# Swin block kernel: the third bf16 part of the attention bias of unshifted blocks as two products of 64 rows

## What is computed

```python
attn = jnp.einsum('bhnd,bhmd->bhnm', q * SCALE, k)
attn = attn + rpb[RPI].transpose(2, 0, 1)[None]
if shifted:
    attn = (attn.reshape(B, NW, HEADS, N, N) + MASK[None, :, None]).reshape(-1, HEADS, N, N)
attn = jax.nn.softmax(attn, -1)
```

## Time and profile before

| | us |
|---|---|
| median of 3 runs | 988.06 |
| lowest and highest | 987.23, 990.0 |
| the profiled execution | 987.27 |
| its span, first to last instruction | 985.4 |
| mean granted TensorE clock in it | 0.865 |
| TensorE busy with products | 796.8 (81%) in 7978 |
| VectorE busy | 794.4 (81%) in 2001 |
| ScalarE busy | 574.2 (58%) |
| GpSimd busy | 244.6 (25%) |

### The profile page before, as it was taken

One profiled execution on the slowest core, in us unless ns is written; L12 is line 12 of the kernel. 1 busy time (PEld: TensorE's weight loads), 2 busy tenths in 40 slices (PEclk: granted clock), 3 DMA queues, 4 the chain that ended last, 5 costly groups with the idle time before them and its releaser, 6 DMA issues.

```text
span 985.4 us, 20394 instructions
## 1 busy us (share of the span) xinstructions
PE 796.8 (81%) x7978; PEld 535.5 (54%) x7980; DVE 794.4 (81%) x2001; ACT 574.2 (58%) x859; POOL 244.6 (25%) x272
## 2 busy tenths in 40 slices
PE   3799999999999999999999979798667655543544
PEld 1577877877777777777777764483111111121222
DVE  8788889988888998888999965744459998989842
ACT  2277777677777777777766663214667636555002
POOL 6122222222222222222222211571201221124100
PEclk8699999999999999999999998799768765565656
DMA  8200000000000000002000000100005666556300
GB/s 225 65 1 3 1 2 2 2 1 3 1 2 2 2 2 1 3 1 103 1 3 2 1 2 4 46 1 0 2 0 97 129 128 126 95 100 128 80 0 17
DMA packets 11621, 34.13 MB, mean 35 GB/s; under 512 B 1879, under 2 KB 4359, under 8 KB 11271
## 3 DMA queue, kind: packets, MB, share of 16 engines
q0 software_dynamic: 5904, 21.24, 11.4%
q1 hardware_dynamic: 5623, 11.60, 4.0%
HBM read 10.81 MB, written 0.79 MB: 12 GB/s over the span
## 4 chain that ended last, share of the span: by engine, by line
PE 62%; DVE 22%; issue 5%; ACT 5%; POOL 2%; DMA 2%; POOLq 0%; SPq 0%; DVEq 0%; ACTq 0%
PE narrow L1453 5%; PE wide L1376 4%; PE scores_a L1425 4%; PE scores_b L1425 4%; PE last L1530 4%; PE scores_a L1412 3%; PE scores_b L1436 3%; PE scores_b L1412 3%; PE scores_a L1436 3%; PE narrow L1483 3%; DVE prod L991 3%; DVE prod L999 2%; PE last L1526 2%; PE wide L1516 2%; PE last L1503 2%
## 5 line engine op out<-in xcount | busy, mean ns | idle before, releaser
L376 POOL TENSOR_TENSOR stb<-stb,neg_half 128x4 f32<-128x4 f32 x48 | 48.4, 1007 | 253.2 <-DVE stb L679 253.2
L1104 ACT ACTIVATE d<-d 128x768 f32<-128x768 f32 x96 | 80.6, 839 | 18.4 <-DVE d L626 17.9
L1453 PEld LDWEIGHTS narrow<-v,pt 128*64 128x64 f32 x2304 | 78.7, 137 | 13.4 <-issue 13.4
L1453 PE MATMUL narrow<-v,pt 128*64 128x54 f32 x2304 | 84.9, 224 | 0.1
L371 POOL TENSOR_TENSOR sta<-sta,neg_half 128x4 f32<-128x4 f32 x48 | 48.9, 1018 | 104.8 <-DVE sta L566 104.8
L1111 ACT ACTIVATE pt<-scores_a 128x768 f32<-128x768 f32 x48 | 38.9, 810 | 56.6 <-PE scores_a L1436 56.6
L1120 ACT ACT_TABLE_LOAD x47 | 60.3, 1283 | 0.8
L1104 ACT ACT_TABLE_LOAD x46 | 59.0, 1283 | 0.8
L613 DVE TENSOR_REDUCE mx<-scores_a 128x12 f32<-128x768 f32 x48 | 46.0, 958 | 16.7 <-PE scores_a L1425 16.7
L1700 PE MATMUL scores_b<-xb,gates_w 128*32 128x512 bf16 x192 | 25.7, 543 | 40.4 <-DVE yo L1013 31.7
L1120 ACT ACTIVATE ga<-wide 128x512 f32<-128x512 f32 x48 | 28.7, 598 | 48.2 <-PE wide L1516 48.2
(11 more groups left out here) (330 smaller groups left out, 2168.2 us busy)
## 6 DMA issues: line engine op xcount, KB each, us to landing
gsum<-mag POOLq DMA_DIRECT2D x14, 512.0 KB, 4.6
ysum<-yo POOLq DMA_DIRECT2D x7, 768.0 KB, 5.8
ysum<-xd POOLq DMA_DIRECT2D x6, 768.0 KB, 5.8
gsum<-mag POOLq DMA_DIRECT2D x14, 256.0 KB, 4.7
wts<-in_wpack SPq DMA_DIRECT2D x6, 442.0 KB, 7.6
sed_w<-in_sed_in SPq DMA_DIRECT2D x1, 2304.0 KB, 8.0
graw<-in_gates_in SPq DMA_DIRECT2D x1, 1152.0 KB, 5.1
x_all<-in_x_tok SPq DMA_DIRECT2D x8, 96.0 KB, 2.9
```

The source lines that it names most:

```text
L1104: act.activation(d, d, ACT.Exp).then_inc(p_ready[u], 1)
L1453: op = pe.matmul(y_ps[64 * b:64 * b + 64, q * VO:(q + 1) * VO], t.pt[:, q, h, 64 * b:64 * b + 64], t.v[:, q, b, h * VO:(h + 1) * VO], star ...
```

## The change

The third part (`bias_lm`) of an unshifted block's bias is now used in products of 64 rows: bank 0 takes rows 0 to 63 of `bias_lm` and of `ident2`, bank 1 rows 64 to 127. So the low part of the second head triple has to lie in rows 64 to 127, where the zeros were: VectorE copies it there behind `table_low` of the even blocks, after a wait for that operation, and the three memsets of zeros on GpSimd are gone. The loops of `bias` are swapped (part outside, bank inside), for shifted blocks too. `tables_done` counts the copies as well, and the counts waited for on it and on `set_v` follow.

```diff
--- before.py
+++ after.py
@@ -39,6 +39,7 @@
 T_COLS = 3456
 L_OFF = [0, 384, 1920, 2304, 3840, 4224]
 L_COLS = 5760
+TABLES = [2, 3, 5, 6, 8, 9]
 
 
 V_PROJ, V_PB, V_PCM, V_F1A, V_F1B, V_F2A, V_F2B, V_GA, V_GC, V_FB, V_YB = (int(n) for n in np.cumsum(
@@ -319,7 +320,7 @@
             for dst, src in ((conv_w[:], conv_in), (l1w[:], l1_in), (l2w[:], l2_in), (front_w[:], front_in),
                              (taps_w[:], taps_in), (l3w[:], l3_in), (spread[:], spread_in)):
                 sp.dma_start(dst, src).then_inc(ld_late, 16)
-            sp.wait_ge(tables_done, BLOCKS)
+            sp.wait_ge(tables_done, TABLES[-1])
             sp.dma_start(sed_w[:], sed_in).then_inc(ld_sed, 16)
             sp.dma_start(signs[:], sign_in).then_inc(ld_sed, 16)
             sp.wait_ge(y_act, CHUNKS)
@@ -352,17 +353,17 @@
             def set_values():
                 for t in st:
                     pool.memset(t.v[:], 0.0).then_inc(set_v, 1)
-                pool.wait_ge(set_v, 5)
+                pool.wait_ge(set_v, 2)
                 for s, t in enumerate(st):
                     for r in range(2):
                         pool.memset(sum_columns(t, r), 1.0).then_inc(set_v, 1)
-                    pool.wait_ge(set_v, 7 + 2 * s)
+                    pool.wait_ge(set_v, 4 + 2 * s)
                 for t in st:
                     pool.memset(t.on[:, :, C:C + 1], 1.0).then_inc(set_on, 1)
                     pool.memset(t.on[:, :, C + 1:64], 0.0).then_inc(set_on, 1)
                 pool.memset(zf[:, :, :, C:C + 1], 1.0).then_inc(set_on, 1)
                 pool.memset(zf[:, :, :, C + 1:64], 0.0).then_inc(set_on, 1)
-                pool.wait_ge(set_v, 9)
+                pool.wait_ge(set_v, 6)
                 pool.wait_ge(set_on, 6)
 
             def rstd_a(n):
@@ -391,9 +392,6 @@
 
             rstd_e(0)
             pool.wait_ge(emb_rstd, 1)
-            for b in (0, 2, 4):
-                pool.memset(bias_lm[64:128, L_OFF[b]:L_OFF[b] + SC], 0.0).then_inc(set_v, 1)
-            pool.wait_ge(set_v, 3)
             for k in range(SLOTS + 4):
                 if k >= 45:
                     rstd_f(k - 45)
@@ -732,6 +730,9 @@
                     low = bias_lm[0:64, L_OFF[b] + w * u:L_OFF[b] + w * (u + 1)]
                     op = dve.tensor_tensor(low, rpb_sb[:, T_OFF[b]:T_OFF[b] + w], low, ALU.subtract)
                 op.then_inc(tables_done, 1)
+                if b % 2 == 0:
+                    dve.wait_ge(tables_done, TABLES[b] - 1)
+                    dve.tensor_copy(bias_lm[64:128, L_OFF[b]:L_OFF[b] + 192], bias_lm[0:64, L_OFF[b] + 192:L_OFF[b] + SC]).then_inc(tables_done, 1)
 
             dve.wait_ge(set_ln, 15)
             embed_centre(0)
@@ -769,7 +770,7 @@
                     fill(2)
                     fill(3)
                 if k == 2:
-                    dve.wait_ge(set_v, 9)
+                    dve.wait_ge(set_v, 6)
                     dve.wait_ge(set_on, 6)
                 take_v(k - 2)
                 take_k(k - 1)
@@ -1394,22 +1395,27 @@
                     return
                 b = n // CHUNKS
                 if n % CHUNKS == 0 and u == 0:
-                    pe.wait_ge(tables_done, b + 1)
+                    pe.wait_ge(tables_done, TABLES[b])
                     if b == 1:
                         pe.wait_ge(ld_mask, 16 * 3)
                 if n >= 1:
                     pe.wait_ge(pt_ready[u], n)
-                for r in range(2):
-                    for part in range(2):
+                for part in range(2):
+                    for r in range(2):
+                        rows = slice(0, 128)
                         if shifted(n):
                             off = (T_OFF[b], L_OFF[b] + 768 * u)[part] + SC * r
                             rhs = (bias_hm, bias_lm)[part][:, off:off + SC]
                             dst = sc_bank[u][:, r, 0:SC]
                         else:
-                            off = (T_OFF[b], L_OFF[b])[part] + 192 * r
-                            rhs = (bias_hm, bias_lm)[part][:, off:off + 192].unsqueeze(1).to_broadcast([128, 2, 192])
+                            if part:
+                                rows = slice(64 * r, 64 * r + 64)
+                                rhs = bias_lm[rows, L_OFF[b]:L_OFF[b] + 192]
+                            else:
+                                rhs = bias_hm[:, T_OFF[b] + 192 * r:T_OFF[b] + 192 * r + 192]
+                            rhs = rhs.unsqueeze(1).to_broadcast([rows.stop - rows.start, 2, 192])
                             dst = sc_bank[u][:, r, 0:SC].rearrange("p (v c) -> p v c", v=2)
-                        pe.matmul(dst, ident2[:], rhs, start=(part == 0), stop=(part == 1))
+                        pe.matmul(dst, ident2[rows], rhs, start=(part == 0), stop=(part == 1))
 
             def scores(n, u):
                 if not live(n):
```

## The result

The changed kernel takes 991.02 us in the median of 22 runs, 989.58 to 997.91; the kernel before, 988.10 us (22 runs, 986.9 to 991.61). The ratio is 1.0037, with a 95% interval of 1.0024 to 1.0050: slower, by 2.4 to 4.9 us. The profiled execution has a span of 990.5 us against 985.4.

The account below looks back on a forecast made before the run. The chain was TensorE for 62% and VectorE for 22%. Terms +2.1 (scores_a), +0.3 (scores_b), +0.3 (half clock) and +0.8 (VectorE copies) sum to +3.5 us; on the median of 988.06 that gives 991.5 us, range 987.6 to 995.8.

Parts of the forecast that it names:

- case A: In TensorE's bias groups, switching between full and partial array costs 0.095 us each way; 989.6 to 992.6 us; chance 0.70.
- The change of the array: On TensorE, each switch between full products and 64-row products costs 0.095 us, twice per bias group.
- Rival B: In the scores_a group, two bf16 64-row products slip between full ones without the drain; 986.7 us; chance 0.13.
- The load of the pair: The weight load in front of the two 64-row products is uncovered for 0.01 us; 0.10 kept for the range.
- rival C: The 64-row weight load loses its short form: +0.09 us in some 43 groups, +3.9, 995.4 us; chance 0.11.
- The load behind the pair: The load for the transposes after the scores_a group adds 0.06 us; bounds 0 and 0.10.
- scores_a pays, scores_b does not: Bias groups: scores_a +0.10 us each; scores_b only +0.015, since the projection behind it waits for VectorE's copy of oT.
- 21 groups: Of 24 unshifted chunks, 21 pay for their groups: scores_a +2.1 us in all, scores_b +0.3 over some 20.
- The copies: Three VectorE copies of 0.27 us: +0.30 in the start-up, +0.25 each for blocks 2 and 4; sum +0.8 us.
- Half clock: Three groups at half clock, where saving doubles and array changes may double too: +0.3 us, bounds -0.3 and +0.4.
- The order, GpSimd, SyncE: Swapping the bias parts, dropping GpSimd's three memsets and SyncE's wait for the last table: 0 us each.
- Rival D: The two halves do not run together in bf16: +0.16 us in 43 groups, +6.9, 998.4 us; chance 0.06.

Follow-up runs that it names:

- pair first: Changed kernel with the pair of 64-row products ahead of the two full products in unshifted groups; 993.01 us, ratio 1.0037 to the kernel before.
- the order: Kernel before with only the bias loops swapped, all products of 128 rows; 987.79 us against 987.93, ratio 0.9996.
- straight to its place: Changed kernel with the pair ahead of the full products and VectorE writing third parts directly in two operations, without a copy; 990.84 us, ratio 1.0033.
- both products on the same half: Changed kernel with both 64-row products on rows 0 to 63, so they can't run together; 1000.72 us, ratio 1.0130 to the kernel before.
- the copies: Kernel before plus the three VectorE copies of 64x192 into a tile nothing reads, bias products as before; 987.53 us against 987.93, ratio 1.0010.
- the pair in one group: Changed kernel with 64-row pairs only in scores_a groups (990.10 us, ratio 1.0035) or only in scores_b groups (989.54 us, ratio 1.0017).

## Why the prediction was right

It gave 991.5 us (987.6 to 995.8); measured were 991.02, and case A is what happened. Point by point:

- **The change of the array, 0.095 us each way: right.** The pair starts 0.26 us after the second full product, and 0.165 of it is that product; the next operation starts 0.26 us after the pair. Rival B is out: no bf16 pair slips in for free. This is the case in which the Trainium skill's page TensorEngine Tiling (Array Packing) is to be read as a whole: its sentence (Key Properties) that a change of tiling mode drains TensorE is borne out in front of all 48 pairs of the profiled execution, and behind those that no wait follows; its speedup of up to two (Theoretical Speedup) was there too (0.16 us a pair) and was smaller than the two drains.
- **The load of the pair, 0.01: right.** Its first product lasts 333 ns against 326; rival C is out.
- **The load behind the pair, 0.06: right**, and shown by itself: with the pair first, 0.05 of it comes back.
- **scores_a pays, scores_b does not: right.** 0.094 and 0.004 us where I had 0.10 and 0.015; the term of +0.3 for scores_b was too large by 0.2.
- **21 groups:** +0.09 to +0.11 in each of 21 chunks at full clock, 2.10 us in all for both groups, where the terms 2.1 and 0.3 stood.
- **The copies: too small, within the bounds.** A copy takes 0.20 us, not 0.27, but the step grows by 0.34 to 0.36, not 0.30: the copy starts 0.03 us after table_low has ended and the next operation 0.03 after the copy, where it used to start 0.08 before the end of table_low. I had counted the 0.03 once and the lost overlap not at all. At n = 11 and 27 that is 0.36 each, where I had 0.25; in the start-up VectorE is 0.34 later, and whether that reaches the end no pair of traces shows. In sum 0.7 to 1.1, where I had 0.8. This and the term for scores_b err in opposite directions, so that the sum of 3.5 is closer than its parts are: 2.10 and these make 2.8 to 3.2.
- **Half clock, +0.3: open in sum, its step shown once.** One group of scores_b lies wholly at the lower clock in both profiles: from its first product to the projection's second pass it is 1.53 us against 1.44, +0.09, where I had about +0.1. The changes there are 0.14 and 0.11, not doubled; the projection's load, covered before and uncovered now, is the rest. For the sum of the three groups: the two executions had different falls of the clock in the start-up, and the chunks there differ by -0.3 to +0.2 us for that reason alone.
- **The order, GpSimd, SyncE: 0**, the order shown by its own run, the others by the trace in which nothing waits for them.
- **Two slips in the numbers.** The range of A begins at 989.8, not 989.6, by its own terms (991.5 - 1.3 - 0.4), and the profiled execution of 987.27 us was not the fastest of the runs shown, of which the lowest is 987.23. Neither changes the forecast, which goes by the median.

Rival D was wrong for the changed kernel and was then built: it gave +12.5 us by the medians, where I had priced it at +10.3. In its profiled execution one chunk, n = 36, costs 3.2 us more than its neighbours, with the clock at its lower level from 455.1 to 461.9.

What the prediction did not have is the clock in the middle of the blocks. It is not needed to explain the slowdown: the clock held there in the profiled executions of before and after alike. But in the profiled executions of the better versions of the change (pair first, straight to its place) it took more, 3.3 us, than the better version gave. What took three runs of the changed kernel to 997.7 us and more is open, since none of them was profiled: such a fall is one candidate, the 3 to 4 us by which the stretch behind the blocks differs from execution to execution another.

These falls are as large as the effect. The mechanism is right, chunk by chunk; that the median of the totals lies within 0.5 us of 991.5 is in part luck.

## What to carry to other kernels

Packing two products of half height saves one product's stream and costs two changes of the array plus the loads that lose their cover; here that is 0.16 against 0.26 us. By these numbers a pair between full products pays only if the product it saves is longer than 0.26 us, or if one of the changes falls into a wait, as in three chunks of the run with the pair first. Next to work that already has that shape it should save a change; no run here shows this. Before shortening a group, look at what releases its neighbour: a product in front of a wait is free, and taking it away gives nothing (0.00 us for the group of scores_b), but only up to the wait's end: what goes beyond it counts in full. A chain of small waits for one engine's rare extra work is worth more than a product in every chunk: spreading it won 2.9 us where the change lost as much.

## What was not expected

Taking work from TensorE made the kernel slower: without the third part 995.0 us in the median against 988.2. In its profiled execution the granted clock fell from 2.4 to 1.2 GHz for 6.8, 10.3 and 6.8 us, each time behind the chunk in which TensorE waited for ScalarE's and VectorE's table work. Spreading that work took the falls away and left 981.5 us. Between the two profiled executions, with the same products, lie 16.3 us of span (998.3 and 982.0), of which 10.4 are the three chunks at the lower clock.

The profiled executions together: falls between 60 and 575 us stand in that of the kernel without the third part (three), of the pair first, of straight to its place and of both products on the same half (one each), all of them 1.3 to 2.5 us behind the end of the wait of 1.05 us for VectorE's table work, the second of the two. None stands in those of the kernels before and after, of the order, of the copies and of the pair in one group, which have the same waits, and none in the three kernels with the table work spread out, which don't. So each of the six falls came behind such a wait, but 24 such waits were followed by none; what decides it in a given execution is open.
